# Four-layer attention and feed-forward kernel: the last attention round in halves, the last layer's normalisation, logits and stores by batch, the gather by 128-column one-hot matrices

## What is computed

```python
# L3 attention: 8 groups of 2 query heads (self and cross), per batch
catq = _div_clamp_fp8(cat, proj_smooth)          # clamp, round to fp8
return jnp.einsum('bsi,oi->bso', catq, wproj) * (proj_in_scale * proj_w_scale)

# L3 feed-forward, on layernorm(x): only k = 32 of a batch's 256 tokens pass through it
logits = (x @ Wr + br)[..., 0]
weights, idx = jax.lax.top_k(logits, k)
...
h = jax.nn.gelu(fx @ W1 + b1, approximate=False)  # fx: the 32 chosen rows, in order of tokens
out_l = h @ W2 + b2
xw = softmax(weights)[..., None] * out_l
return x.at[bidx, tokens].add(xw)
```

## Time and profile before

| | |
|---|---|
| median of 3 runs | 1182.13 us (1180.92 to 1184.97) |
| profiled execution, its own time | 1181.37 us |
| its span in the profile | 1179.3 us |
| busy TensorE / weight loads | 1027.8 / 876.6 us |
| busy VectorE / ScalarE / GpSimd | 860.0 / 626.6 / 543.2 us |
| mean granted TensorE clock | 0.934 of full |

### The profile page before, as it was taken

One profiled execution on the slowest core, in us unless ns is written; L12 is line 12 of the kernel. 1 busy time (PEld: TensorE's weight loads), 2 busy tenths in 40 slices (PEclk: granted clock), 3 DMA queues, 4 the chain that ended last, 5 costly groups with the idle time before them and its releaser, 6 DMA issues.

```text
span 1179.3 us, 18867 instructions
## 1 busy us (share of the span) xinstructions
PE 1027.8 (87%) x6460; PEld 876.6 (74%) x6460; DVE 860.0 (73%) x2157; ACT 626.6 (53%) x1653; POOL 543.2 (46%) x408
## 2 busy tenths in 40 slices
PE   4999999999994978878479599999999999999936
PEld 4648888888883765555346488898889898999825
DVE  4437777777778536488986688988887888888653
ACT  1474444444332343678746457665767666666510
POOL 2316766677652222001245465556555656555520
PEclk9899999999997998888698799999999999999966
DMA  6002011011000101000000101010101000000011
...
DMA packets 13630, 37.13 MB, mean 31 GB/s; under 512 B 1296, under 2 KB 5472, under 8 KB 12896
## 3 DMA queue, kind: packets, MB, share of 16 engines
...
...
## 4 chain that ended last, share of the span: by engine, by line
PE 73%; DVE 13%; ACT 7%; issue 4%; POOL 1%; DMA 1%; SPq 0%; DVEq 0%; POOLq 0%; ACTq 0%
PE bank L677 15%; PE bank L2028 9%; PE bank L2016 9%; PE bank L1993 7%; PE bank L697 7%; PE bank L2040 4%; PE bank L1951 4%; PE bank L1038 2%; PE bank L1965 2%; PE bank L1053 1%; PE bank L487 1%; PE bank L488 1%; DMA cxT<-in_dram 1%; PE bank L1249 1%; DVE bst L240 1%
## 5 line engine op out<-in xcount | busy, mean ns | idle before, releaser
L2131 ACT ACTIVATE y<-bank,g_mx 128x256 f32<-128x256 f32 x256 | 117.2, 484 | 101.1 <-DVE g_mx L2272 87.9
L2368 POOL TENSOR_TENSOR y<-y,g_sm 128x1024 f32<-128x1024 f32 x64 | 119.8, 1893 | 21.8 <-DVE g_sm L2280 21.8
L2345 POOL TENSOR_TENSOR g_c<-arena 128x1024 fp32r<-128x1024 f32 x32 | 68.3, 2134 | 128.6 <-DVE arena L2250 128.6
L2016 PE MATMUL bank<-arena 128*128 128x256 f32 x512 | 116.0, 379 | 0.0
L715 ACT ACTIVATE arena<-arena 128x512 f32<-128x512 f32 x64 | 40.4, 632 | 125.6 <-DVE arena L796 125.5
L2016 PEld LDWEIGHTS bank<-arena 128*128 128x128 f32 x512 | 95.0, 190 | 11.9 <-issue 0.2
L677 PE MATMUL bank<-b_yh,b_wh 128*128 128x512 f32 x256 | 102.0, 398 | 0.0
L677 PE MATMUL bank<-b_yl,b_wh 128*128 128x512 f32 x256 | 101.4, 396 | 0.0
L677 PE MATMUL bank<-b_yh,b_wl 128*128 128x512 f32 x256 | 101.1, 395 | 0.0
L1993 PE MATMUL bank<-g_qh,g_xs 128*128 128x256 f32 x256 | 69.4, 306 | 22.3 <-POOL g_xs L2332 15.8
L750 POOL TENSOR_TENSOR b_hl<-arena,b_hh 128x512 fp32r<-128x512 f32 x64 | 81.3, 1291 | 10.3 <-ACT b_hh L724 10.3
...
## 6 DMA issues: line engine op xcount, KB each, us to landing
...
arena<-in_dram SPq DMA_DIRECT2D x17, 256.0 KB, 4.0
arena<-in_dram SPq DMA_DIRECT2D x3, 1024.0 KB, 7.8
cx<-in_dram SPq DMA_DIRECT2D x2, 1024.0 KB, 7.5
...
x<-in_dram SPq DMA_DIRECT2D x1, 1024.0 KB, 5.7
cxT<-in_dram SPq DMA_DIRECT2D x1, 1024.0 KB, 11.7
out_dram<-x SPq DMA_DIRECT2D x1, 1024.0 KB, 4.4
```

The source lines that it names most:

```text
L2016: m = pe.matmul(o[:, st * 256:st * 256 + 256], g_t[:, c, st * P:st * P + P], keys, start=True, stop=True)
L2131: m = act.activation(g_p[:, c, st, :], o[:, st * 256:st * 256 + 256], ACT.Exp, bias=g_mx[j % 2][:, 2 * c + st:2 * c + st + 1], accum_out=g ...
L2345: pool.tensor_tensor(cat, g_o[j % 2], g_om, ALU.subtract).then_inc(s_gc, 1)
L2368: pool.tensor_tensor(pf, pf, sums, ALU.mult).then_inc(s_gp, 1)
```

## The change

- `G_end_pe`, `G_end_act`, `G_end_dve`, `G_end_pool` replace steps 33 to 35 of the pipeline. VectorE copies pt 0 and pt 2 of round 31 one after the other, then rounds 30, then 31 in two halves of 512 columns (`G_ob_dve`, the halves with a buffer `h_om` of their own), and only then adds round 30. GpSimd subtracts in the same halves, and the projection of round 31 takes the first half's columns first.
- Normalisation of the last layer, by batch: batch 0's statistics in step 32 between the two reciprocals, those of 1, 2 and 3 behind the additions that complete them, the scalings between, into a new place `h_y`. In TensorE's list the transposes and the logits alternate.
- The set-up of the router's weights, and a memset of the one-hot tiles (128x1024), go to step 32. `W2` and `W1` are loaded when round 31's queries and round 28's P·V are done.
- The search has no copy, the positions need one operation less behind the scan, chosen slots are masked by adding 1024, and the exponential masks by -1e30 and sums in the same instruction. Only the slots are transposed ahead of the gather; the weights after it.
- One-hot tiles are 128 columns wide (32 slots of each batch); each of the eight comparisons signals by itself. The gather is 8 matmuls with the one-hot tile stationary and 256 columns of `h_y`, so it gives slots by values; it is copied (`h_fs`), transposed (`fx`) and copied again. ScalarE copies the transposed one-hots in two pieces, GpSimd adds `h_y` to `x` in four pieces, and the spreading matmuls use all 128 rows.
- Each batch is stored when added (256 KB), without the markers.
- In every round the wait for GpSimd's subtraction stands ahead of the clamp and no longer behind it.

```diff
+        def G_end_pe(pe):
+            j = NG - 1
...
+            o = claim(pe, ("G", "pj", j))
+            for half in range(2):
+                pe.wait_ge(s_gc, j + 1 + half)
+                for st in range(2):
+                    for c in (2 * half, 2 * half + 1):
+                        for w in (g_ph, g_pl):
+                            m = pe.matmul(o[:, st * D:st * D + D], g_c[j % 2][:, c, st * P:st * P + P],
+                                          w[j // B % 2][:, c, :], start=(half == 0 and st == 0 and c == 0 and w is g_ph),
+                                          stop=(c == 3 and w is g_pl), skip_group_check=True)
+            fill(m, ("G", "pj", j))
...
+        def G_ob_dve(dve, V, j, om, cs=slice(0, 1024)):
+            ob = g_ob[j % 2][:, cs]
+            V.do(dve.tensor_scalar(ob, ob, FP8_MAX, -FP8_MAX, ALU.min, ALU.max))
+            V.sync()
+            V.do(dve.tensor_scalar(om[:, cs].bitcast(U16), ob.bitcast(U16), 0x7F80, None, ALU.bitwise_and))
+            V.sync()
+            V.do(dve.tensor_scalar(om[:, cs], om[:, cs], FP8_TINY, FP8_MAGIC, ALU.max, ALU.mult))
+            V.sync()
+            dve.tensor_tensor(g_o[j % 2][:, cs], ob, om[:, cs], ALU.add).then_inc(s_gt, 1)
+        def G_end_dve(dve, V):
+            j = NG - 1
+            G_add_dve(dve, j - 2)
+            for c in G_PT_DVE:
+                G_pt_dve(dve, j, c)
+            have(dve, ("G", "pv", j - 1, 0))
+            have(dve, ("G", "pv", j - 1, 1))
+            dve.wait_ge(s_gc, j - 1)
+            G_ob_dve(dve, V, j - 1, g_om)
+            for a in range(2):
+                have(dve, ("G", "pv", j, a))
+                G_ob_dve(dve, V, j, h_om, slice(512 * a, 512 * a + 512))
+            have(dve, ("G", "pj", j - 2))
+            ln_open_batch(dve, V, 1)
+            ln_scale(dve, K_H, 0)
+            G_add_dve(dve, j - 1)
+            have(dve, ("G", "pj", j - 1))
+            ln_open_batch(dve, V, 2)
+            ln_scale(dve, K_H, 1)
+            G_add_dve(dve, j)
+            have(dve, ("G", "pj", j))
+            ln_open_batch(dve, V, 3)
+            ln_scale(dve, K_H, 2)
+            ln_scale(dve, K_H, 3)
...
+                    if i == NG and tt == 0:
+                        have(dve, ("G", "pj", NG - B))
+                        ln_open_batch(dve, V, 0)
+                        H_setup_dve(dve, V)
...
+        def G_end_pool(pool, C):
+            j = NG - 1
+            ln_pool(pool, C, K_H, EPS, batches=(0,))
+            pool.wait_ge(s_gt, j)
+            take(pool, ("G", "pj", j - 3))
+            pool.tensor_tensor(g_c[(j - 1) % 2][:, :, :].rearrange("p c s -> p (c s)"), g_o[(j - 1) % 2], g_om,
+                               ALU.subtract).then_inc(s_gc, 1)
+            take(pool, ("G", "pj", j - 2))
+            for a in range(2):
+                pool.wait_ge(s_gt, j + 1 + a)
+                cs = slice(512 * a, 512 * a + 512)
+                pool.tensor_tensor(g_c[j % 2][:, 2 * a:2 * a + 2, :].rearrange("p c s -> p (c s)"), g_o[j % 2][:, cs],
+                                   h_om[:, cs], ALU.subtract).then_inc(s_gc, 1)
+            ln_pool(pool, C, K_H, EPS, batches=range(1, B))
+            for b in range(B):
+                pool.wait_ge(s_y, 2 * ln_at[(K_H, b)] + 2)
+                xb = x[:, 2 * b:2 * b + 2, :]
+                pool.tensor_tensor(xb, xb, h_y[:, 2 * b:2 * b + 2, :], ALU.add).then_inc(s_hxy, 1)
...
+            plan(("H", "yt", b), b % 2)
...
         def H_sp(sp):
-            sp.wait_ge(s_stage, 6)
+            take(sp, ("G", "q", NG - 1, 1))
+            sp.dma_start(h_w2, W2_d).then_inc(s_hw2, 16)
+            take(sp, ("G", "pv", NG - B, 1))
             sp.dma_start(h_w1, W1_d).then_inc(s_hw1, 16)
-            sp.dma_start(h_w2, W2_d).then_inc(s_hw2, 16)
+            for b in range(B):
+                sp.wait_ge(s_hx, b + 1)
+                have(sp, ("H", "add", b))
+                sp.dma_start(out_d[b].rearrange("(h p) d -> p h d", p=P), x[:, 2 * b:2 * b + 2, :]).then_inc(s_out, 16)
+            sp.wait_ge(s_out, 16 * B)
+        def H_logits_pe(pe, b, o):
+            have(pe, ("H", "yt", b))
+            for k in range(KD):
+                m = pe.matmul(o[0:B, 0:256], h_wr[:, k, b * B:b * B + B], h_xT[:, k, b * 256:b * 256 + 256],
+                              start=(b == 0 and k == 0), stop=(b == B - 1 and k == 1), skip_group_check=True)
+            if b == B - 1:
+                fill(m, ("H", "lg"))
 
         def H_pe(pe):
-            yt_pe(pe, K_H, "H")
+            yt_pe(pe, K_H, "H", LOW)
             pe.wait_ge(s_hwr, 1)
             o = claim(pe, ("H", "lg"))
...
+            H_logits_pe(pe, 0, o)
+            yt_pe(pe, K_H, "H", (2,))
+            H_logits_pe(pe, 1, o)
+            yt_pe(pe, K_H, "H", (3,))
+            H_logits_pe(pe, 2, o)
+            H_logits_pe(pe, 3, o)
             o = claim(pe, ("H", "pT"))
             pe.wait_ge(s_hpos, 1)
...
+            for q in range(2):
+                m = pe.transpose(o[:, q * B:q * B + B], h_pos[0:B, q * P:q * P + P], ident[0:B, 0:B])
-            o = claim(pe, ("H", "fx"))
-            pe.wait_ge(s_hoh, 1)
-            for d in range(KD):
-                for b in range(B):
-                    for q in range(2):
-                        m = pe.matmul(o[:, d * P + b * SLOTS:d * P + b * SLOTS + SLOTS],
-                                      y[:, 2 * b + q, d * P:d * P + P], h_oh[:, 2 * b + q, :],
-                                      start=(q == 0), stop=(q == 1))
-            fill(m, ("H", "fx"))
+            o = claim(pe, ("H", "fs"))
+            for t in range(T):
+                pe.wait_ge(s_hoh, t + 1)
+                m = pe.matmul(o[:, 0:D], h_oh[:, t, :], h_y[:, t, :], start=(t == 0), stop=(t == T - 1))
+            fill(m, ("H", "fs"))
+            o = claim(pe, ("H", "eT"))
+            pe.wait_ge(s_hew, 1)
+            for q in range(2):
+                m = pe.transpose(o[:, q * B:q * B + B], h_ew[0:B, q * P:q * P + P], ident[0:B, 0:B])
+            fill(m, ("H", "eT"))
             for c in range(2):
                 o = claim(pe, ("H", "ohT", c))
                 for j in range(4):
-                    m = pe.transpose(o[0:SLOTS, j * P:j * P + P], h_oh[:, 4 * c + j, :], ident)
+                    m = pe.transpose(o[:, j * P:j * P + P], h_oh[:, 4 * c + j, :], ident)
                 fill(m, ("H", "ohT", c))
+            o = claim(pe, ("H", "fx"))
+            have(pe, ("H", "fs"))
+            for k in range(KD):
+                m = pe.transpose(o[:, k * P:k * P + P], h_fs[:, k * P:k * P + P], ident)
+            fill(m, ("H", "fx"))
...
             for b in range(B):
                 o = claim(pe, ("H", "add", b))
-                r = 32 * b
                 for q in range(2):
-                    m = pe.matmul(o[:, q * D:q * D + D], h_ohT[r:r + 32, q, :], h_out[r:r + 32, :],
-                                  start=True, stop=True)
+                    m = pe.matmul(o[:, q * D:q * D + D], h_ohT[:, 2 * b + q, :], h_out, start=True, stop=True)
                 fill(m, ("H", "add", b))
 
...
-            yt_act(act, "H")
+            for b in range(B):
+                o = take(act, ("H", "yt", b))
+                empty(act.copy(h_xT[:, :, b * 256:b * 256 + 256], o[:, :].rearrange("p (d n) -> p d n", d=KD)),
+                      ("H", "yt", b))
             act.wait_ge(s_hmx, 1)
-            act.activation(h_ew[0:B, :], h_lg[0:B, :], ACT.Exp).then_inc(s_hex, 1)
+            act.activation(h_ew[0:B, :], h_lg[0:B, :], ACT.Exp, bias=h_sm[0:B, 2:3], accum_out=h_sm[0:B, 0:1])\
+                .then_inc(s_hex, 1)
+            for c in range(2):
+                o = take(act, ("H", "ohT", c))
+                empty(act.copy(h_ohT[:, 4 * c:4 * c + 4, :], o[:, :].rearrange("p (t n) -> p t n", t=4)),
+                      ("H", "ohT", c))
             for c in range(2):
...
+            V.do(dve.tensor_tensor(h_not[b4, :], left[b4, :], h_lg[b4, :], ALU.is_equal))
+            V.do(dve.tensor_tensor(h_sel[b4, :], left[b4, :], h_lg[b4, :], ALU.not_equal))
+            V.do(dve.tensor_scalar(h_sm[b4, 2:3], h_m8[b4, 0:1], -1.0, None, ALU.mult))
+            V.sync()
+            dve.scalar_tensor_tensor(out=h_lg[b4, :], in0=h_not[b4, :], scalar=-BIG, in1=h_lg[b4, :],
+                                     op0=ALU.mult, op1=ALU.add).then_inc(s_hmx, 1)
+            V.do(dve.tensor_tensor_scan(h_pos[b4, :], b_z[b4, :], h_sel[b4, :], -1.0, ALU.add, ALU.add))
+            V.sync()
+            dve.scalar_tensor_tensor(out=h_pos[b4, :], in0=h_not[b4, :], scalar=1024.0, in1=h_pos[b4, :],
+                                     op0=ALU.mult, op1=ALU.add).then_inc(s_hpos, 1)
             dve.wait_ge(s_hex, 1)
             V.do(dve.reciprocal(h_sm[b4, 1:2], h_sm[b4, 0:1]))
...
             have(dve, ("H", "pT"))
             for t in range(T):
-                m = dve.tensor_scalar(h_oh[:, t, :], cst[:, 264:296], h_pT[:, 0, t % 2, t // 2:t // 2 + 1], None,
```

(23 more changed lines are left out.)

210 lines of the change are left out of this document (99 added, 111 removed).

## The result

The changed kernel takes **1165.98 us** (median of 4 runs, 1164.22 to 1166.61) against 1181.95 for the kernel before on the same chip: ratio 0.986, 95% interval 0.9843 to 0.9877. The forecast was 1167.8, with a range of 1161 to 1173. The profiled execution took 1166.6 us, its span is 1164.8, its mean clock 0.944.

A forecast was written before the change was run, and what follows sets the result against it. The prediction took a chain of waits handed between engines through the tail as the bound. Its terms, -8.9 - 2.5 - 1.0 + 0.3 - 0.1 - 2.1 = -14.3, gave 1167.1 from 1181.37, then 1167.8 for the median; range 1161 to 1173.

The forecast's parts named there:

- term 1: End of the attention to the logits: new order, halves and normalisation by batch end the logits earlier, -8.9 us.
- term 6: Final store: only the last 256 KB store, taken at 2.7 us, remains behind the last addition, -2.1 us.
- The holding of the two masks: Last rounds: VectorE's mask operations stretch beside GpSimd's subtractions, the one in round 31's first half to near 2 us.
- term 2: Top-32 search to the gather's first matmul: fewer operations and a start behind the first one-hot operation, -2.5 us.
- Term 3: The gather: 16 instructions of 256 columns, with the clock returning 5 us in, take 6.0 instead of 7.00, -1.0 us.
- term 4: Gather to the first layer: more transposes and a copy in a row, 2.0 us instead of 1.71, +0.3 us.
- Term 5: Final additions: VectorE starts 0.3 earlier but is fed 0.06 late each time, -0.1 us.
- Rival A: TensorE's clock drops between the logits, costing 2.2 in term 1 and slowing gather and transposes: 1172 us, chance 0.22.
- C: Clock falls ahead of projection 30 and never returns, everything behind at half: 1188 us, chance 0.03.
- B: No holding: VectorE's halves slip between GpSimd's operations, term 1 is -11 to -12.7: 1164 to 1165 us, chance 0.25.
- D: The gain goes into waits in VectorE's stretch and four stores take as long as one: 1176 to 1180 us, chance 0.05.

The follow-up runs named there:

- late: Changed kernel, but GpSimd's residual additions all wait for the last scaling instead of each for its own batch: 1162.95 us, ratio 0.9827.
- t1all: Changed kernel with round 31 whole, its rounding behind round 30's addition, and the last normalisation as one block: 1174.11 us, ratio 0.9938.
- narrow: Changed kernel with the gather again as 32 instructions of 32 columns, without the first copy and the rows' two transposes: 1168.86 us, ratio 0.9884.
- best2: Changed kernel with late's waiting residual additions and 14 extra matmul calls, whose result nobody reads, during the search: 1162.53 us, ratio 0.9835.
- subdve: Changed kernel with the last three subtractions (round 30 and round 31's halves) on VectorE instead of GpSimd: 1166.05 us, ratio 0.9852.
- whole: Changed kernel with round 31 rounded, subtracted and projected whole, not in halves: 1166.30 us, ratio 0.9864.
- oldorder: Changed kernel with VectorE adding round 30 again before it rounds round 31: 1169.72 us, ratio 0.9898.
- lnend: Changed kernel with the whole last normalisation again behind the last addition: 1169.35 us, ratio 0.9899.

## Why the prediction was right, and where its terms were off

- **The sum** was -14.3, the two spans differ by 14.5. That they agree so well is luck: term 1 was 1.25 too large; the stretch ahead of the tail (-0.9, within the scatter) and term 6 (-0.5) made up for it.
- **The medians** differ by 16.0, since the profiled execution took 0.6 more than its median after the change and 0.6 less before. The tails differ by 13.6 only, so some 2.4 lie ahead of the tail, or in tails that weren't profiled. Median less tail is 1114.8 for the kernel before and 1111.1 to 1113.1 for the thirteen others. The wait that moved in every round, put at 0, may have gained there; no run separates it from the scatter.
- **Term 1**, -8.9 against -7.65. The holding of the two masks came as walked (2.11 and 1.21), and the unheld 512-wide operations took 0.29 and 0.69 where I took 0.30 and 0.65. Mis-sized was the last pair of scalings: "each of the last two scalings may wait for one: 1130.2 to 1132.1, I take 1131.3". Both waited; put on the time base of before it ended at 1132.2, the upper end. `late` shows that this one conflict costs 1.9 us on VectorE and 1.7 at the search. The other 0.3 lies in transposes and logits, 2.6 instead of 2.3.
- **What made term 1** I had walked as one order of events without sharing it out. `t1all` shows that without order, normalisation by batch and halves nothing of it is left, and that they aren't additive.
- **Terms 2, 3 and 4** hit within 0.1. Of term 2, the 1.1 for starting behind the first one-hot operation is confirmed (1.0 in `narrow`). Term 3 was luck in part: with the return of the clock "5 us into it" I got 6.0, but the same instructions took 5.14 to 6.66 in other executions. And a second effect of the wide gather, a first layer wholly at the full clock, is in no term: it is the -0.2 of the two layers, and 1.5 in `narrow`. The clock came back 3.5 us into the dense transposes of the kernel before, and not 3.3 as I read it; no term hangs on that.
- **Term 5** is +0.2 and not -0.1. VectorE doesn't start 0.3 earlier: its first addition starts 1.71 behind the bias, before 1.72. And the eight additions take 3.40 instead of 3.23, since VectorE waits up to 0.37 between them for TensorE. **Term 6**: the stores land in 2.2 (median of four) and not 2.7, near the smaller bound. The estimate by the Trainium skill, "DMA: Bandwidth & Descriptors", section "Anatomy of one DMA", was 2.6 for it; the measurement, on this kernel's queue, is 0.4 below. The single store, 4.5, agrees with the 4.4 that the page's figures give.
- **Rival A** (the clock drops between the logits) didn't occur in the profiled execution, but its first half did in those of `late`, `best2` and `subdve`, whose windows within 1120 to 1130 fall below 1.00. It cost nothing at the search there and not 2.2, because VectorE paces that stretch and the clock was back by the last batch: from the last batch's first transpose to the search it is 2.5 in all four. **C** wanted a clock that falls ahead of projection 30 and never returns: it stayed full there in all 13 profiles, and where gaps of 2.6 to 5.7 us ahead of later work (`whole`, `oldorder`, `lnend`, `t1all`) did drop it, that work brought it back. **B** is out: the mask took 2.11 (by its own terms its time was 1164.0 to 1165.7). **D** is out: TensorE has no gap between projection 29 and the transposes behind the memset, and GELU waits 0.87 for TensorE, not for its table.
